# Mixing stage in two parts, recurrence steps between its matmuls, split expert outputs, last stage's additions on VectorE

## What is computed

```python
xn = layernorm(x)                      # L0: both branches read xn
#   recurrent branch
y = layernorm(xn) * ln_w + ln_b
u = y @ Ws.T + bs + y @ Wi.T + bi      # 16 states per token
h_t = tanh(h_{t-1} @ A.T + u_t)        # along the 2048 tokens
s = (H @ Wo.T + bo) * sigmoid(y @ Wg.T + bg) + xn
#   gate branch: 64 small networks of 16 relu units each
g = silu((sum_h(relu((xn @ Win + bin) * W1 + b1) * W2) + b2) @ Wout + bout)
x = x + s * g
# L1: attention over the 4 batches at each token, and top-2 of 8 experts
x = x + attention(layernorm(x)) * silu(moe(layernorm(x)))
```

## Time and profile before

| | us |
|---|---|
| median of 3 runs (1509.65 to 1512.31) | 1510.79 |
| the profiled execution | 1510.5 |
| its span, first to last instruction | 1508.7 |

### The profile page before, as it was taken

How to read it: one execution, slowest core, us unless ns; L and a number is a source line. 1 busy time by engine, 2 the same in 40 slices (tenths; PEclk the granted TensorE clock), 3 DMA queues, 4 the chain that set the end, 5 groups by cost and what they waited for, 6 DMA issues and landing times. The chain is left out here.

```text
span 1508.7 us, 23107 instructions
## 1 busy us (share of the span) xinstructions
PE 1219.6 (81%) x7479; PEld 811.8 (54%) x7479; DVE 1007.7 (67%) x1829; ACT 619.5 (41%) x933; POOL 684.8 (45%) x577
## 2 busy tenths in 40 slices
PE   2999997758888888433899999999899999999800
PEld 1655664436666666312466666666566665666500
DVE  2777774035888888787567756667666765676547
ACT  0555553223444444100545544554544454464321
POOL 2122220003777777701345554454555544555559
PEclk9999998659999999755899999999999999999955
DMA  9000002300000001010655555464455545556577
GB/s 309 1 0 0 0 0 114 165 15 29 29 29 29 29 29 30 15 56 22 144 82 96 106 106 98 70 133 82 89 107 106 109 65 130 85 90 106 77 199 258
DMA packets 156359, 122.20 MB, mean 81 GB/s; under 512 B 88400, under 2 KB 147664, under 8 KB 154864
## 3 DMA queue, kind: packets, MB, share of 16 engines
q1 hardware_dynamic: 116128, 77.61, 17.5%
q0 software_dynamic: 25200, 35.85, 16.6%
q10 hardware_dynamic: 14944, 7.62, 1.8%
HBM read 58.91 MB, written 44.30 MB: 68 GB/s over the span
## 5 line engine op out<-in xcount | busy, mean ns | idle before, releaser
L1652 ACT ACTIVATE e_h_all<-e_pH,e_b1c,e_h_scale 128x512 f32<-128x512 f32 x256 | 199.7, 780 | 279.3 <-PE e_pH L1693 277.2
L1707 PE MATMUL e_pY<-e_w_hi,e_h_hi 128*128 128x256 f16 x1024 | 281.2, 275 | 12.8 <-DVE e_w_lo L1527 12.6
L1451 POOL DMA_INDIRECT expert_sums<-e_yo,e_dcol x128 | 210.5, 1644 | 168.1 <-DVE e_yo L1605 132.8
L1709 PE MATMUL e_pY<-e_w_hi,e_h_lo 128*128 128x256 f16 x1024 | 280.7, 274 | 0.0
L1708 PE MATMUL e_pY<-e_w_lo,e_h_hi 128*128 128x256 f16 x1024 | 280.6, 274 | 0.0
L1437 POOL DMA_INDIRECT e_xg<-xn_rows,e_icol x140 | 161.8, 1156 | 195.9 <-DVE e_icol L1468 163.1
L1570 DVE TENSOR_TENSOR e_h_lo<-e_h_all,e_h_hi 128x512 f16<-128x512 f32 x256 | 176.9, 691 | 61.6 <-ACT e_h_hi L1652 48.9
L1691 PE MATMUL e_pH<-e_xT,e_w_hi 128*128 128x512 f16 x512 | 195.8, 382 | 22.1 <-DMA e_xT<-e_xs 15.4
L1692 PE MATMUL e_pH<-e_xT,e_w_hi 128*128 128x512 f16 x512 | 195.8, 382 | 0.0
L1693 PE MATMUL e_pH<-e_xT,e_w_lo 128*128 128x512 f16 x512 | 195.5, 382 | 0.0
L1707 PEld LDWEIGHTS e_pY<-e_w_hi,e_h_hi 128*128 128x128 f16 x1024 | 100.7, 98 | 37.6 <-DVE e_h_lo L1570 19.7
(11 more groups left out here) (231 smaller groups left out, 2235.9 us busy)
## 6 DMA issues: line engine op xcount, KB each, us to landing
raw<-expert_w SPq DMA_DIRECT2D x18, 1024.0 KB, 6.2
expert_sums<-r_zero SPq DMA_DIRECT2D x10, 1024.0 KB, 12.7
xn_rows<-c_xn SPq DMA_DIRECT2D x16, 512.0 KB, 3.0
f_ya<-expert_sums SPq DMA_DIRECT2D x16, 512.0 KB, 5.6
out<-f_ya SPq DMA_DIRECT2D x16, 512.0 KB, 3.9
x_st<-x ACTq DMA_DIRECT2D x4, 1536.0 KB, 13.9
e_xg<-xn_rows,e_icol POOLq DMA_INDIRECT x140
e_xT<-e_xs SPq DMA_TRANSPOSE x136
```

The source lines that it names most:

```text
L1451: pool.indirect_dma_start(v.y_dram, bass.IndirectOffsetOnAxis(dcol[u][:, q:q + 1], axis=0), yo[:, q, :], None, bounds_check=N + CAP - 1, o ...
L1652: last = act.activation(dst, pH[h % NPH][:, :], ACT.Relu, bias=b1c[eu][:, h:h + 1], scale=h_scale[eu][:, 0:1])
L1707: pe.matmul(pY[:, q, :], h_hi[:, h, cols], w2_hi[:, h, :], start=(h == 0), stop=False)
L1709: last = pe.matmul(pY[:, q, :], h_lo[:, h, cols], w2_hi[:, h, :], start=False, stop=(h == HT - 1))
```

## The change

**Loads.** x now comes in four parts of four tiles, each with its own semaphore, all on SyncE's queue: two parts in prepare, two in mix, and behind them late and b1t. ScalarE's queue no longer issues any of x.

**mix in two parts.** The first part goes over all tiles and does statistics, one normalisation, turning and the recurrence's input alone. Statistics run four tiles ahead, GpSimd makes scales for two tiles at once; of the four batches VectorE normalises one and ScalarE three. The turned tile goes to prod_st, which is free until then, and pT and pG take turns as its PSUM, pS and pGU as that of the input. The second part waits for all of u_st and does the rest of the tile from prod_st; for finish, VectorE normalises every tile a second time. After a tile's gate, its unit sums, the next tile's inner sums and its pZ stands one step of the recurrence each (slots 0 to 3), so tiles 0 to 11 hold the 48 steps. A step is now two matmuls into a bank half of pT: identity times u_st, and the state's. VectorE's comparison is at tiles 9, 13 and 15. The transfers of zeros are issued once the first part's evictions are done, from a source of 1 KB a partition that is read eight times.

**recur** keeps the flag's test and the further sweeps.

**experts.** y_done, yb_ready and weighted count halves of two blocks; VectorE makes the gate first, then adds and multiplies half by half; GpSimd scatters two blocks a half.

**combine.** VectorE does the addition too; GpSimd has no work.

```diff
+def load_x(eng, v, n):
+
+    for b in range(B):
+        rows = v.x[b, n * FIRST * P:(n + 1) * FIRST * P, :]
+        eng.dma_start(v.x_st[:, n * FIRST:(n + 1) * FIRST, b * D:(b + 1) * D],
+                      rows.rearrange("(t p) d -> p t d", p=P)).then_inc(v.x_in[n - 1], 16)
...
-                sp.dma_start(v.late[:, :], v.late_w[:, 0:L_B1]).then_inc(v.late_in, 16)
-                sp.dma_start(v.b1t[:, :], v.late_w[:, L_B1:L_ALL]).then_inc(v.late_in, 16)
+                load_x(sp, v, 1)
...
-                act.wait_ge(v.x_first, 16 * B)
-                for b in range(B):
-                    act.dma_start(v.x_st[:, FIRST:, b * D:(b + 1) * D],
-                                  v.x[b, FIRST * P:, :].rearrange("(t p) d -> p t d", p=P)).then_inc(v.x_in, 16)
...
+        turned = [pT[:, :, :].rearrange("p k c -> p (k c)"), pG[:, :, :].rearrange("p b d -> p (b d)")]
+        pU = [pS, pGU]
+        pR = [pT[:, n, 0:NCH] for n in range(2)]
...
+        def xnT(t):
+            return v.prod_st[:, t, :].rearrange("p (k c) -> p k c", k=KD)
+
+        def steps_at(t, slot):
+
+            j = SLOTS * t + slot
+            return [(j, j // L, j % L)] if j < SWEEPS * L else []
...
-                sp.wait_ge(v.late_in, 32)
+                for n in range(2, NT // FIRST):
+                    load_x(sp, v, n)
+                sp.dma_start(v.late[:, :], v.late_w[:, 0:L_B1]).then_inc(v.late_in, 16)
+                sp.dma_start(v.b1t[:, :], v.late_w[:, L_B1:L_ALL]).then_inc(v.late_in, 16)
+                sp.wait_ge(cleared, 1)
+                sp.wait_ge(t_evac, NT)
+                parts = (N + CAP) // (P * 8)
+                for n in range(parts):
+                    rows = slice(n * P * 8, (n + 1) * P * 8)
+                    sp.dma_start(v.y_dram[rows, :].rearrange("(p r) d -> p r d", p=P),
+                                 zero[:, :].unsqueeze(1).broadcast_to([P, 8, D])).then_inc(zeroed, 16)
+                sp.wait_ge(zeroed, 16 * parts)
...
+                for k in range(NT // PAIR):
+                    ts = slice(PAIR * k, PAIR * k + PAIR)
+                    pool.wait_ge(stats, PAIR * (k + 1))
+                    pool.tensor_tensor(ta[:, :, :], mv[:, ts, :, 1], eps[:, :, :], ALU.add).then_inc(rchain, 1)
+                    pool.tensor_tensor(tb[:, :, :], mv[:, ts, :, 0], mone[:, :, :], ALU.mult).then_inc(rchain, 1)
+                    pool.wait_ge(rchain, 5 * k + 2)
+                    pool.tensor_tensor(r1[:, ts, :], ta[:, :, :], mhalf[:, :, :], ALU.pow).then_inc(r_ready, 1)
+                    pool.wait_ge(r_ready, k + 1)
+                    pool.tensor_tensor(nmr[:, ts, :], tb[:, :, :], r1[:, ts, :], ALU.mult).then_inc(nmr_ready, 1)
...
+                def first_rows(t):
+                    dve.wait_ge(r_ready, t // PAIR + 1)
+                    if t >= 2:
+                        dve.wait_ge(t_done, t - 1)
+                    dve.tensor_scalar(xn[t % 2][:, 0, :], v.x_st[:, t, 0:D], mv[:, t, 0, 0:1], r1[:, t, 0:1],
+                                      ALU.subtract, ALU.mult).then_inc(first_xn, 1)
...
+                for t in range(FIRST):
+                    measure(t)
+                first_rows(0)
+                for t in range(NT):
+                    if t + FIRST < NT:
+                        measure(t + FIRST)
+                    if t + 1 < NT:
+                        first_rows(t + 1)
+                    if t:
+                        take_u(t - 1)
+                take_u(NT - 1)
...
+                dve.wait_ge(t_done, NT)
+                normalise(0)
+                units(0)
+                for t in range(NT):
...
+                    if t:
+                        finish(t - 1)
+                    if t + 1 < NT:
+                        if t:
+                            dve.wait_ge(x_done, t)
+                        normalise(t + 1)
...
+                def rows(t):
+                    act.wait_ge(nmr_ready, t // PAIR + 1)
+                    if t >= 2:
+                        act.wait_ge(t_done, t - 1)
+                    for b in range(1, B):
+                        last = act.activation(xn[t % 2][:, b, :], v.x_st[:, t, b * D:(b + 1) * D], ACT.Identity,
+                                              scale=r1[:, t, b:b + 1], bias=nmr[:, t, b:b + 1])
+                    last.then_inc(xn_ready, 1)
...
+                for t in range(NT):
+                    rows(t)
+                    if t:
+                        take_turned(t - 1)
+                take_turned(NT - 1)
...
+                def step(t, slot):
+                    for j, n, l in steps_at(t, slot):
+                        act.wait_ge(summed, j + 1)
+                        if j == SWEEPS * L - 1:
+                            act.wait_ge(saved, 1)
+                        act.activation(v.h_st[:, l, :], pR[j % 2], ACT.Tanh, bias=v.u_bias[:, 0:1]).then_inc(state, 1)
...
+                take_s(0)
+                units(0)
+                for t in range(NT):
+                    step(t, 0)
+                    act.wait_ge(y_ready, t + 1)
+                    act.activation(v.prod_st[:, t, :], v.prod_st[:, t, :], ACT.Tanh, scale=0.5).then_inc(thy_ready, 1)
                     act.wait_ge(kan_done, t + 1)
+                    act.activation(gT[:, :], pGU[:, :], ACT.Identity, bias=v.gconst[:, 0:1]).then_inc(gT_ready, 1)
+                    step(t, 1)
+                    if t + 1 < NT:
+                        take_s(t + 1)
+                    step(t, 2)
+                    if t + 1 < NT:
+                        units(t + 1)
                     act.wait_ge(z_done, t + 1)
-                    act.activation(gT[:, :], pGU[:, :], ACT.Identity, bias=v.gconst[:, 0:1]).then_inc(gT_ready, 1)
-                    if more:
-                        evac(t + 1)
-                    act.wait_ge(y_ready, t + 1 + 1)
-                    act.sem_inc(passed, 1)
-                    act.activation(v.prod_st[:, t, :], v.prod_st[:, t, :], ACT.Tanh, scale=0.5).then_inc(thy_ready, 1)
...
+                def step(t, slot):
+                    for j, n, l in steps_at(t, slot):
+                        if j:
+                            pe.wait_ge(state, j)
+                        ins = pe.matmul(pR[j % 2], ident, v.u_st[:, l, :], start=True, stop=(j == 0),
+                                        skip_group_check=True)
+                        if l:
+                            ins = pe.matmul(pR[j % 2], v.at_blk, v.h_st[:, l - 1, :], start=False, stop=True,
+                                            skip_group_check=True)
+                        elif n:
+                            ins = pe.matmul(pR[j % 2][:, 1:NCH], v.at_blk, v.h_st[:, L - 1, 0:NCH - 1],
+                                            start=False, stop=True, skip_group_check=True)
+                        ins.then_inc(summed, 1)
+
...
+                pe.wait_ge(u_evac, NT)
+                pe.wait_ge(v.late_in, 32)
+                inner(0)
+                for t in range(NT):
+                    if t:
...
+                    step(t, 0)
...
+                    step(t, 1)
+                    if t + 1 < NT:
+                        inner(t + 1)
+                    step(t, 2)
+                    if t:
+                        pe.wait_ge(sf_ready, t)
...
+                    step(t, 3)
...
-                sweep(0, first=True)
-                for n in range(1, SWEEPS):
-                    sweep(n)
...
-                        pool.wait_ge(weighted, n + 1)
-                        pool.sem_inc(passed, 1)
                         for q in range(BLK):
+                            if q % 2 == 0:
+                                pool.wait_ge(weighted, 2 * n + q // 2 + 1)
+                                pool.sem_inc(passed, 1)
...
-                    dve.wait_ge(y_done, n + 1)
-                    if g == 0:
-                        dve.wait_ge(b2_in[eu], 8 * (e - eu) + 16)
-
-                    dve.scalar_tensor_tensor(yo[:, :, :], pY[:, :, :], y_scale[eu][:, 0:1],
-                                             b2b[eu].unsqueeze(1).broadcast_to([P, BLK, D]),
-                                             ALU.mult, ALU.add).then_inc(yb_ready, 1)
...
+                    for m in range(2):
+                        part = yo[:, 2 * m:2 * m + 2, :]
+                        dve.wait_ge(y_done, 2 * n + m + 1)
+                        dve.sem_inc(passed, 1)
+                        dve.scalar_tensor_tensor(part, pY[:, 2 * m:2 * m + 2, :], y_scale[eu][:, 0:1],
+                                                 b2b[eu].unsqueeze(1).broadcast_to([P, 2, D]),
+                                                 ALU.mult, ALU.add).then_inc(yb_ready, 1)
+                        dve.wait_ge(yb_ready, 2 * n + m + 2)
+                        dve.tensor_tensor(part, part, gate[g][:, 2 * m:2 * m + 2].unsqueeze(2).broadcast_to([P, 2, D]),
+                                          ALU.mult).then_inc(weighted, 1)
...
+                        if q % 2:
```

(7 more changed lines are left out.)

335 lines of the change are left out of this document (145 added, 190 removed).

## The result

The changed kernel takes **1450.09 us** (median of 4 runs, 1442.77 to 1451.42) against 1510.22 (4 runs, 1508.83 to 1512.31): ratio 0.9591, 95% interval 0.9557 to 0.9625. It is faster, and 3.5 us under the forecast of 1453.6. The profiled execution took 1449.93 us, its span 1448.0. The sum comes out better than its terms: two of them missed by 7 and 10 us in opposite directions.

The account below looks back on a forecast made before the run. Bounds: TensorE in mixing and experts, handovers in the recurrence, VectorE and GpSimd in the last stage, DMA near full. Gains 42.5 + 1 + 2.5 + 10.9 = 56.9 from 1510.5 gave 1453.6 us, range 1444 to 1474.

Parts of the forecast that it names:

- Entry: Start of mixing: without ScalarE's issues of x, the first statistics start at 13.8, 12.2 us earlier.
- Part one: First part of mixing: VectorE has most to do, a turn is 3.1 us, 54.6 in all, ending about 68.4.
- Part two: Second part of mixing: TensorE bounds at 11.3 us a tile plus 0.47 a step, 203.4 us, then a 4.7 drain.
- the upper end, 0.95: Recurrence step in mixing's second part: at most a full handover, 0.46 wait for the tanh plus 0.49 matmul.
- Part one at 1.2 GHz: Rival: TensorE's clock is low in mixing's first part, about 11 us more, up to 13; time 1465, chance 0.14.
- I take 1: Experts' stage: VectorE's shorter tail cuts TensorE's waits, a gain between nothing and 12.6 us, taken as 1.
- The splitting itself costs two more starts of VectorE a group, in its cover: Experts' stage: VectorE's two extra starts a group fit beside TensorE's work, so no cost was added.
- The 12.6: Experts' stage: TensorE's only repeating wait, for VectorE, 12.6 us in 16 pieces, taken as the most to gain.
- The 2.5 us at the end of the stage: End of the experts: GpSimd's idle 2.80 us before its first scatter shrinks to 0.30, a gain of 2.5.
- Last stage: VectorE without GpSimd beside it takes 2.5 us a tile; gain 10.9 us, midway between 8.9 and 12.8.
- the lower end: Final stage: the DMA engines move 16.8 MB at 322 GB/s in 52.1 us, a gain of only 8.9.
- The sum: Whole kernel: gains of 42.5 before attention, 1 and 2.5 in the experts and 10.9 at the end, 56.9 us.

Follow-up runs that it names:

- steps in one place: The changed kernel with the four recurrence steps of a tile issued together behind the gate's matmuls, instead of at four places in the tile: 1478.25 us.
- doubled: The changed kernel with the first matmul of each recurrence step issued twice, the result being the same: 1458.20 us.
- experts-in-one-piece run: The changed kernel with the whole experts' stage put back as before the change, its output in one piece: 1438.82 us.

## Why the prediction was right

The time is right, and so are the bounds named for each stage but the experts'; that the sum came so close is in part luck.

**Entry.** Forecast 13.8, measured 13.32; with ScalarE's queue filled again, all of it goes.

**Part one: mis-sized, right bound.** The term was a turn of 3.1 us; 2.55 was measured. From start to start the statistics go at 1.70 a tile (not 1.95), the quarter at 0.30 (not 0.35) and the input at 0.55 (not 0.81). Some 0.30 of the difference is overlap, which adding durations misses: aggregation, quarter and product each take 0.05 to 0.16 less until the next one starts than was counted. The other 0.25 is idle time in the rows of before that was counted in and shrank here: 0.18 ahead of the aggregation to 0.03, and 0.42 from the copy's start to the product's to 0.32. Twelve turns and the lead give 7.6 us less, and 2.2 come back at the end (four turns without statistics and the last input). Part one ended at 62.5, not 68.4.

**Part two.** 11.3 and 0.47 were forecast, 11.11 and 0.44 measured; TensorE's list is 199.1 us long against 203.4, the end behind it 5.5 against 4.7. That the other matmuls cover the tanh is shown by the runs with steps in one place and doubled. Taking the share of four records as a step's price was right, and the upper end, 0.95, was too low: 1.17.

**Part one at 1.2 GHz** (the first in the list of rivals, though called the second ahead of it). It did not happen. By the rule of the Trainium skill that the prediction quotes (TensorE: Matmul & The Clock Gate, section HAM oscillation — how this bites in real kernels) the clock would stay high here, and it did, at 1.00; but with the lead of one tile it fell behind gaps of 3.1 to 3.8 us, and with the steps in one place it fell at times at gaps of 0.46 us, in part two at a mean of 0.98. Here gaps of 0.67 us left it high, so their length alone doesn't decide.

**Experts: the term that was wrong.** "I take 1" of TensorE's 12.6 us of waits, and "The splitting itself costs two more starts of VectorE a group, in its cover". The bounds were a gain of nothing to 12.6; a loss was not excluded by any row and should have been an end of the range. The 12.6 were also not the right upper end: the row names e_w_lo, weights that VectorE prepares, and the waits for it stayed, 11.1 us in 14 pieces. The starts cost nothing that shows. What the split moved is GpSimd's scatters, to the passage between two groups, and no step priced them. The change is 11.5 us slower than the same kernel with its scatters held (1446.8 and 1435.3 on one chip); between traces 8 to 13 us of the experts' stage go with it (708.2 and 710.2 against 697.4 to 700.0), though the two first traces, with the clock's falls in the one of before, show only 6.3. The 2.5 us at the end of the stage came as forecast.

**Last stage.** 12.7 against 10.9, with an upper end of 12.8. Midway between two limits was too careful: the lower end was taken from 322 GB/s, a rate seen while VectorE and GpSimd held the stores back, and without them 365 flow.

**The sum** was off by only 3.5 us because -9.8 ahead of attention and -1.8 at the end nearly cancel with +7.3 in the experts. That is luck.

## What to carry to other kernels

A chain of short dependent steps costs only its own matmuls once it is spread through a stage that has other work on the same engine: here 0.44 us a step in place of 1.17 where they follow one another. Place the steps apart, and price a handover with all the matmuls that stand in it. When a result is handed on in halves, ask what the first half's consumer will now do in the middle of the producer's work; here early scatters cost 8 to 13 us inside the stage and won 1 to 2 us at its end, and holding them back beats both kernels, at 0.9506 to 0.9517 of the time of before.

## What the runs showed of the hardware that was not expected

- With an indirect scatter under way on GpSimd as a group's last output matmul ends, or started up to 0.7 us behind it, ScalarE and VectorE mostly start their next work, for which they wait on TensorE, about 2 and 3 us late: in the trace of the change ScalarE 3.2 to 3.5 us behind TensorE's start in place of 1.5, VectorE mostly 3.2 to 3.5 in place of 0.3 to 1.0 with the scatters held. Scatters that start 1.1 us or more behind it do no harm. In nine traces with early scatters the experts' matmuls took 708.2 to 717.8 us, in four with later ones 697.4 to 700.0.
- The same stage in the same code took 703.9 us in the kernel before and 698.2 in the experts-in-one-piece run, mostly for three short falls of the clock in the former. One profiled execution does not tell such 6 us from a cost.
- Short VectorE instructions can overlap in the records: the aggregation of 0.38 us is followed at 0.29, the normalisation of 0.38 at 0.30 and the product of 0.39 at 0.23 us from start to start. A group of statistics of 1.38 is followed at 1.41.
